# One more unit of layer 2 is split, its low part on GpSimd, and the split units stand at every second place

## The reference

```
def _cin(x, Ws, bs):                       # x: (1024, 39, 16)
    h, outs = x, []
    for i, (W, b) in enumerate(zip(Ws, bs)):
        L, Fk = W.shape[-1], h.shape[1]    # L = 128; Fk = 39, then 64, 64
        z = einsum('bfd,bgd->bfgd', x, h)
        cur = relu(einsum('bfgd,fgl->bld', z, W.reshape(39, Fk, L)) + b[None, :, None])
        h, direct = cur[:, :64], cur[:, 64:]   # the last layer: all of cur is direct
        outs.append(direct)
    return concatenate(outs, axis=1).sum(-1)
...
h = relu(concatenate([z, dense_ctx], axis=1) @ W_top1 + b_top1)
y = relu(h @ W_top2 + b_top2) @ W_top3
```

## Time and profile before

| what | before |
|---|---|
| median of 3 runs (range) | 1365.14 us (1364.8 to 1367.58) |
| the profiled execution | 1367.65 us, span 1366.0 us |
| TensorE busy | 1247.5 us, 91% of the span |
| VectorE busy | 1044.1 us, 76% |
| GpSimd busy | 998.2 us, 73% |
| ScalarE busy | 727.2 us, 53% |

### The profile page before, as it was taken

How to read it: one execution, slowest core, us unless ns; L and a number is a source line. 1 busy time by engine, 2 the same in 40 slices (tenths; PEclk the granted TensorE clock), 3 DMA queues, 4 the chain that set the end, 5 groups by cost and what they waited for, 6 DMA issues and landing times.

```text
span 1366.0 us, 15702 instructions
## 1 busy us (share of the span) xinstructions
PE 1247.5 (91%) x3980; PEld 729.5 (53%) x3980; DVE 1044.1 (76%) x944; ACT 727.2 (53%) x943; POOL 998.2 (73%) x607
## 2 busy tenths in 40 slices
PE   0025999999999999999999999999999999999999
PEld 0012565555555555655555555556555555655545
DVE  0115878899888888888898788888888988889731
ACT  2102556656655565556566555655565666556432
POOL 6770368898888888888888888888888865556511
PEclk9996999999999999999999999999999999999999
DMA  8097256667766656666776656666576766655000
GB/s 172 11 182 148 46 121 125 131 136 141 140 130 124 122 116 122 123 122 131 136 140 140 137 119 119 120 123 128 115 129 137 140 138 138 132 121 141 1 0 1
DMA packets 101052, 160.50 MB, mean 117 GB/s; under 512 B 17322, under 2 KB 29467, under 8 KB 100845
## 3 DMA queue, kind: packets, MB, share of 16 engines
q1 hardware_dynamic: 90715, 156.66, 56.4%
q0 software_dynamic: 10240, 2.74, 2.0%
HBM read 155.47 MB, written 6.19 MB: 118 GB/s over the span
## 4 chain that ended last, share of the span: by engine, by line
PE 51%; POOL 22%; issue 20%; another core or an unknown queue 3%; DVE 2%; ACT 2%; DMA 1%; POOLq 0%; DVEq 0%; ACTq 0%
PE curM L757 25%; POOL zl L261 12%; POOL emb L250 9%; PE curM L774 7%; PE curM L766 6%; PE curM L767 6%; PE curY L757 4%; DVE z L474 2%; PE h L842 2%; ACT h L624 1%; PE xk L842 1%; PE curY L842 1%; PE curY L767 0%; PE curY L766 0%
## 5 line engine op out<-in xcount | busy, mean ns | idle before, releaser
L261 POOL TENSOR_TENSOR zl<-z,zh 128x1024 fp32r<-128x1024 f32 (+1 forms) x281 | 673.6, 2403 | 277.1 <-ACT zh L607 267.3
L474 DVE TENSOR_TENSOR z<-xr,h 128x1024 f32<-128x1024 f32 x576 | 668.7, 1211 | 23.4 <-PE curM L757 13.9
L757 PE MATMUL curM<-z,wf 128*128 128x512 f32 (+2 forms) x1290 | 585.0, 602 | 17.6 <-issue 17.6
L607 ACT ACTIVATE zh<-z 128x1024 fp32r<-128x1024 f32 (+1 forms) x352 | 367.9, 1054 | 295.1 <-DVE z L474 252.7
L250 POOL DMA_INDIRECT emb<-in_tbl_dram,idx x312 | 319.1, 1023 | 70.2 <-issue 59.5
L766 PE MATMUL curM<-zh,wl 128*128 128x512 f32 (+1 forms) x642 | 345.5, 538 | 11.9 <-ACT zh L607 9.9
L757 PEld LDWEIGHTS curM<-z,wf 128*128 128x128 f32 (+2 forms) x1290 | 227.8, 189 | 230.5 <-issue 208.8
L525 DVE TENSOR_TENSOR zl<-z,zh 128x1024 fp32r<-128x1024 f32 (+1 forms) x71 | 136.7, 1925 | 175.7 <-ACT zh L607 175.7
L767 PE MATMUL curM<-zh,wh 128*128 128x512 f32 (+1 forms) x642 | 252.2, 393 | 0.0
L774 PE MATMUL curM<-zl,wh 128*128 128x512 f32 (+1 forms) x642 | 205.1, 401 | 5.6 <-POOL zl L261 4.5
L766 PEld LDWEIGHTS curM<-zh,wl 128*128 128x128 f32 (+1 forms) x642 | 121.7, 189 | 86.4 <-issue 50.5
(11 more groups left out here) (94 smaller groups left out, 372.1 us busy)
## 6 DMA issues: line engine op xcount, KB each, us to landing
xr<-xT SPq DMA_DIRECT2D x384, 192.0 KB
xs<-xT SPq DMA_DIRECT2D x96, 546.0 KB
xq<-xT SPq DMA_DIRECT2D x64, 256.0 KB
emb<-in_tbl_dram,idx POOLq DMA_INDIRECT x312
xT<-xc SPq DMA_DIRECT2D x32, 78.0 KB
xr<-in_L_rec_W_dram SPq DMA_DIRECT2D x16, 144.0 KB
xT<-xc SPq DMA_DIRECT2D x32, 40.0 KB
xs<-in_W_top_dram SPq DMA_DIRECT2D x2, 512.0 KB, 6.5
```

What stands on the lines that cost most here:

```text
L261: nc.gpsimd.tensor_tensor(zl[0:n, SNUM[r, u] % NL, :], z[0:n, z_slot(r, u), :], zh[0:n, SNUM[r, u] % NH, :], ALU.subtract).then_inc(lo_poo ...
L474: return nc.vector.tensor_tensor(z[:, slot, :].rearrange("p (a n) -> p a n", a=2), x, h, ALU.mult)
L607: nc.scalar.activation(zh[0:n, SNUM[r, u] % NH, :], z[0:n, z_slot(r, u), :], ACT.Copy).then_inc(hi_ready, 1)
L757: mm = nc.tensor.matmul(cur[:, :], wf[rows, full_at(u), a, :], z[rows, z_slot(r, u), a * N:(a + 1) * N], start=start and i == 0, stop=stop ...
```

## The change

One string changes. Of layer 2 (units 10 to 19), units 16 and 18 become full, and units 15, 17 and 19 become split with the low part on GpSimd. A full round has then 12 split units in place of 11, ten of them with the low part on GpSimd in place of nine, and 12 full ones in place of 13. The unit of VectorE's low part, 14, stays.

```
-KINDS = "GFGFDGFGFF" + "FGFGDFGFGF" + "FGFF"
+KINDS = "GFGFDGFGFF" + "FGFGDGFGFG" + "FGFF"
```

## The result

The changed kernel takes **1408.6 us** at the median (4 runs, 1405.26 to 1410.45) against 1365.45 before (4 runs): **1.031 times the time before, 95% interval 1.0287 to 1.0333**. The forecast was 1398 in 1380 to 1412, slower with a chance of 0.93. The side and the place were right; the loss was larger by 10 us than the likeliest case.

What follows compares the result with a forecast made beforehand. GpSimd's run between the subtractions of units 7 and 21 bounds gather rounds, TensorE the others. 31.0 + 4.2 - 2.8 = +32.4 us on the profiled 1367.65 gives 1400.0, at the median 1398; range 1380 to 1412.

Steps and rivals of the forecast that it cites:

- The bound: Rounds with gathers: GpSimd's run from unit 7's subtraction to unit 21's has no pause to spare; without gathers TensorE bounds.
- Ten-gather rounds: GpSimd's added subtraction makes unit 21's low part late on TensorE: +1.72 us in each of 18 rounds, +31.0.
- half of it: Rival, 10%: the gather behind unit 13's subtraction loses its extra 0.80 us and nine-gather rounds come in time; 1377 us.
- Nine-gather rounds: GpSimd's subtraction of unit 15 collides with VectorE's of unit 14: +0.7 us in each of six rounds, +4.2.
- Rounds without gathers: GpSimd has time there and TensorE alone counts; one full unit less saves 0.35 us, eight times, -2.8.
- GpSimd's slack carries it: Rival, 5%: GpSimd works ahead using its pause before unit 5's subtraction, leaving only TensorE's 0.35 saving; 1354 us.
- The clock: Rival, 8%: TensorE's new waits lower its granted clock in gather rounds, +18 to +36 us more, 1416 to 1434.

## Why the prediction was right in its side and short in its size

**The bound.** Right: a gather round is GpSimd's run from S7 to S21 plus a fixed rest. The two kernels that shorten that run and keep GpSimd's work show it, and the kernel that puts the tenth subtraction into the pause shows that the count alone is not the cause.

**Ten-gather rounds, +1.72 each, +31.0.** Right. They are 39.05 to 39.33 long where 39.1 was forecast; S15 to S21 stand 3.53 apart where 3.54 was, and S14 and the gather behind S13 met as before. The gather took the 0.80 more that "half of it" would have taken away.

**Nine-gather rounds, +0.7 each, +4.2: this is the step that failed.** I took the longest subtraction of GpSimd in the earlier trace rows, 3.367 us, for what S15 would cost when VectorE's S14 comes in between S13 and S15. It did not come in between: GpSimd went straight on, S15 took its usual time, and S14 waited for both. The 3.367 came from a case in which it did. Its rows, in the trace of before, are two subtractions of GpSimd back to back and VectorE's between them:

```profile
1271.44 2.37 POOL L261 TENSOR_TENSOR zl<-z,zh 128x1024 fp32r<-128x1024 f32 x1 [4.30 <-ACT zh L607]
1273.76 3.37 POOL L261 TENSOR_TENSOR zl<-z,zh 128x1024 fp32r<-128x1024 f32 x1
...
1272.35 2.54 DVE L525 TENSOR_TENSOR zl<-z,zh 128x1024 fp32r<-128x1024 f32 x1 [3.42 <-ACT zh L607]
```

There VectorE had been issued 0.91 us behind the start of the first subtraction; in the nine-gather rounds it was 0.09 to 0.13. I took a row of one order for the other.

That the loser of this port blocks to the end, for which I cited the Trainium skill (SBUF — State Buffer, the section on two separate sides), agrees with the trace in either order: 3.37 is a subtraction that waited for VectorE's to end, and 5.71 is two subtractions (4.74 less 0.13) and 1.10, about a free one of VectorE's own. That VectorE was passed over when the first of the two ended goes beyond what I cited. What I had wrong is who comes next, and so what is late next: not S15 but the product of unit 17, and behind it S17. I also took 0.80 off because the gather would no longer meet S14; it met it all the same, one place later, and took 1.77. (That the gather is longer for the same reason as a subtraction is not shown by any run; that it is longer beside VectorE's subtraction is.) In numbers, S15 to S17 took 2.37 + 1.77 + 1.48 = 5.6 us where I had 3.37 + 0.97 = 4.3: 1.3 more in each of six rounds, 7.8 us. Measured from S7 to S7, a nine-gather round is 1.95 longer than before where I had 0.7. The sums for the profiled pair differ by 40.3 - 32.4 = 7.9; the other terms are off by 0.5 or less each.

The gather rounds add up. From the first S7 of the gather rounds to the last it took 1063.91 - 202.08 = 861.8 us before and 1103.81 - 200.50 = 903.3 now, 41.5 more: the 17 ten-gather periods are 1.75 longer on the mean, 29.8, and the six nine-gather ones 1.95, 11.7.

**Rounds without gathers, -0.35 each.** Right in round 0 (0.36 shorter) and from lo21 of round 25 to that of round 28, 36.65 us a round where it was 36.99. From there to the end of the span it takes 128.9 us where it took 130.0: 1.1 less, for two rounds and the last layer 2. Round 25 is 0.5 longer, not shorter: ScalarE waits 5.87 us for the last gather to land, and lo2 comes 0.74 late. In the kernel with a gather between S13 and S15 and in the one with VectorE's subtraction one unit later, that gather stands at the same place, the wait is 4.41 and 4.48, and the round is 36.65 and 36.63. So this 0.5 belongs to one gather that landed late in this execution, and the forecast holds in round 25 of those two.

**GpSimd's slack carries it (5%).** Its mechanism was sound at another place: with the gathers in the pause the same work gives 1354 us, which is the very time that this rival named: its gather rounds are 37.0 to 37.1 us, the saving of 0.35 below those of before. As the kernel stood, the slack lay ahead of S5 and could not be used for S21.

**The clock (8%).** It did not fall in rounds 1 to 24. The 1.5 us of half clock that I priced for a fall were the width of the stretch that I had asked for in the earlier trace rows, not a measured length, so the price stays open.

## What to carry to other kernels

Take an engine's slack where it lies: find the place in the round where the engine must wait for something that another does at a fixed place (here the transpose), and count the work from there to the first deadline, since a pause behind the deadline pays for nothing ahead of it. When an instruction is inserted, look what then stands back to back on the same engine; a small step between two long ones may have been the gap through which another engine got a shared resource. And a change that loses may be right in itself: the split saves TensorE 0.34 us in a round where GpSimd holds nothing up, and paid as soon as two gathers of a ten-gather round, and one of a nine-gather round, left the run from S7 to S21.

## What the runs showed of the hardware that I had not expected

Two GpSimd subtractions back to back kept VectorE's subtraction of two SBUF operands waiting through both: issued 0.13 us behind the start of the first it took 5.71 us, where one with a gather behind the first took 3.35. The other order occurs as well, in every one of the twelve traces. Of all cases in which VectorE's subtraction was issued while the first of two back-to-back GpSimd subtractions ran, it waited through both in the 24 in which it was issued 0.08 to 0.13 us behind the first one's start. In the 19 in which it was issued 0.32 to 2.10 us behind, it came in between, and the second of GpSimd took 3.35 to 3.41. The offset goes with the outcome in all 43; no run changed the offset alone, so that it decides is not shown.

The wait of 1.34 us for GpSimd near 154 us is in the changed kernel's trace too (at 154.38), but there the clock stayed at 1.00 in 154.5 to 156, where it was 0.50 before. Of the twelve profiled executions of this study four show a half clock at that place. The transposes behind it come 1.2 us earlier than before (156.67 against 157.89), and with the 0.36 of round 0 that is the 1.6 us by which the first S7 of the gather rounds comes earlier. It is not tied to the change: of the four, one has the units of before and three have twelve split units.
